# q and k of the second attention stored once in single precision, and split into high and low parts where they are used

## The chip, the core and the metric

The kernel runs on one core of a Trainium2 chip. The metric is the device time of one execution in microseconds. Five engines work side by side, each through its own queue in order: TensorE (PE; its weight loads are shown apart as PEld), VectorE (DVE), ScalarE (ACT), GpSimd (POOL) and SyncE (SP), which here only issues DMAs. They wait for each other by semaphores.

## What is computed

Two layers over 4 sequences of 1024 tokens of width 128. Each layer is an attention with 16 heads and a feed-forward part, both with a residual and a layer norm. The change touches the second attention alone:

```python
q = (x @ Wq).reshape(B, T, H, D)      # B 4, T 1024, H 16, D 64
k = (x @ Wk).reshape(B, T, H, D)
v = (x @ Wv).reshape(B, T, H, D)
q = _rmsnorm(q, q_rms_w)
k = _rmsnorm(k, k_rms_w)
gate = jax.nn.softplus(jnp.einsum('bthd,hd->bht', k, u_n) / math.sqrt(D))
bias = -dist[None, None] * omega_eff[None, :, None, None] * gate[:, :, None, :]
bias = jnp.where(causal[None, None], bias, -jnp.inf)
scores = jnp.einsum('bihd,bjhd->bhij', q, k) * scale + bias
attn = jax.nn.softmax(scores, axis=-1)
y = jnp.einsum('bhij,bjhd->bihd', attn, v).reshape(B, T, H * D)
return y @ Wproj
```

## The kernel before

All tensors are single precision. For q·k the kernel splits each value into a high part, rounded to a type that TensorE multiplies in one pass (`F32R`), and a low part, the rounded rest. The product is then high·high, plus low·high and high·low.

**The projection of the second attention** is the last part of `middle` (`sync_last`, `tensor_last`, `vector_last`, `scalar_last`, lines 1685 to 2014). It goes over 96 items in order: for each of 32 tiles of 128 tokens the items q, k and v. Four tiles are a chunk; there are 8 chunks. Every engine goes through the same numbers n:
- TensorE: `multiply(n)` (line 1783, the product in one of three pairs of banks), then, for item n-3 if it is q or k, two groups of four transposes ("half", line 1742) into one of two banks. After n = 4 of a chunk come the four `aug` transposes of the gates (line 1756), and after n = 8 those of the next chunk's input and the small gate products (lines 1746 and 1752). The two banks are handed on by `free` (line 1759): for a half, when `lower` has read it (semaphore `lows`).
- ScalarE: `root3(n-1)`, then `square(n)` or `keep_v(n)`, then for item n-3 `higher` twice (line 1972), which writes the half times the norm's weight, rounded, into `high`. At n = 2 `soften` (two exponential steps with table loads) for the chunk before, at n = 4 `keep_aug`.
- VectorE: `scale(n-1)` (lines 1843 to 1852), then for item n-3 `lower` twice (line 1864: the half times the weight, minus `high`, into `low`), then `reduce(n)` (line 1836). At n = 3 the gates, at n = 5 `join` and at n = 7 `norm` of the next chunk.
- SP stores `high` and `low` of each q and k item to `s_q1` and `s_k1`, 512 KB each, v to `s_v1`.

**The second attention** is `attend_and_finish`. It goes over `G` = 32 pairs of heads (4 sequences of 8 pairs). A pair has 12 steps u (`units`), each of up to 512 queries against 128 keys: the first four for queries 0 to 511, the other eight for queries 512 to 1023. Steps go in runs of four. For a run TensorE does `scores` of its four steps (lines 564, 565 and the mask, 567), each step followed by `jobs` of the next pairs, and then `values` of the four steps (line 580).
- A job "max" multiplies 128 queries with up to 512 keys (line 537, high parts only) into one of 3 banks (`RING`). VectorE takes the row maximum (lines 631 and 634). `share` says how many jobs follow each step: 3, 2, 1, 1, then 2 each and so on; from step 8 they belong to pair g+2. The maxima of a pair are joined (line 638), transposed (540), negated (640) and laid by a DMA from the ACT queue as one row of `QA` (line 695). `ahead` is what is done before the first score: all maxima of pair 0 and nine of pair 1.
- `scores` writes into 4 banks (`NE`); a step wider than 256 queries takes a bank for each head. ScalarE's `exponentials` (line 690) read them into a ring of 8 `prob` buffers. GpSimd adds these up for the denominators (lines 731 to 735). `keep` (702) and `keep_den` (671) on ScalarE take outputs and denominators out of their banks.
- Operands: `QA` and `KA` hold the high parts in rows 0 to 63 and the position, slope and maximum rows behind them, in 4 buffers (`NA`). `QB` and `KB` hold high and low parts on 128 rows, in 3 buffers (`NB`). `load_a` brings k high, q high and the slopes, `load_b` the four parts for `KB` and `QB` and V. Each of these q and k loads is 512 KB, so a pair takes six of them. A buffer is loaded again when the values of its pair are done.

After the last pair comes the output projection with the last feed-forward part, whose weights and inputs are laid over buffers of the attention that are done with (`over`, `load_last`).

## Time and profile before

| | us |
|---|---|
| median of 3 runs | 2565.62 (2562.55 to 2566.68) |
| the profiled execution | 2563.43 |
| its span, first to last instruction | 2561.3 |
| TensorE busy | 2217.8 |
| VectorE busy | 1378.8 |
| ScalarE busy | 1141.2 |
| GpSimd busy | 682.6 |
| mean granted TensorE clock | 0.922 of 2.4 GHz |

All durations come from the one profiled execution. A granted clock of 0.50 is 1.2 GHz. The projection of the second attention runs from about 873 to 1304 us, the second attention from 1317 to 2151.

### The profile page before, as it was taken

The page shows a single profiled execution, that of the slowest core. Times are in us where ns is not written, and L with a number is a line of the kernel's source. Part 1 is how long each engine was busy: PE and PEld are TensorE (multiplying, and loading weights), DVE is VectorE, ACT ScalarE, POOL GpSimd, SP SyncE. Part 2 cuts the span into 40 slices and gives each one's busy share as a digit, 9 for nine tenths or more (in the row PEclk, how much of TensorE's full clock was granted, in tenths as well). Part 3 has the DMA queues.
Part 4 walks back from the last instruction along what each step waited for, and adds up shares of the span by engine and source line. Part 5 has one row for each costly group of instructions (what it writes and reads, how often), then busy time and mean ns, then how long its engine had stood idle before and what let it go on. Part 6 is the DMA issues. An engine that isn't in the chain of part 4 may idle for free. (4 is left out here: it accounts for less than half of the span.)

```text
span 2561.3 us, 33066 instructions
## 1 busy us (share of the span) xinstructions
PE 2217.8 (87%) x11088; PEld 1286.7 (50%) x11088; DVE 1378.8 (54%) x3484; ACT 1141.2 (45%) x1838; POOL 682.6 (27%) x463
## 2 busy tenths in 40 slices
PE   5499999999839667766749999999999998599998
PEld 2244444444538434333326565656556565355554
DVE  3476766766343476767655555556555553333321
ACT  2145555555525355555534444544444443132322
POOL 5000000000140200000006767676676665000000
PEclk8799999999759888887859999999999999799999
DMA  5724333422227476766698777878787875525300
GB/s 174 201 79 116 128 122 125 92 64 55 93 70 200 115 221 183 216 207 200 200 230 181 172 168 167 175 160 179 163 177 162 181 183 157 141 75 138 84 9 9
DMA packets 339126, 369.66 MB, mean 144 GB/s; under 512 B 22280, under 2 KB 260872, under 8 KB 338573
## 3 DMA queue, kind: packets, MB, share of 16 engines
q1 hardware_dynamic: 321920, 338.45, 52.7%
q0 software_dynamic: 7344, 24.21, 2.7%
q10 hardware_dynamic: 9696, 4.92, 0.8%
q8 instruction: 89, 1.46, 0.3%
q14 instruction: 77, 0.62, 0.1%
HBM read 219.19 MB, written 147.79 MB: 143 GB/s over the span
## 5 line engine op out<-in xcount | busy, mean ns | idle before, releaser
L690 ACT ACTIVATE a1prob<-ps 128x512 f32<-128x512 f32 (+2 forms) x640 | 328.8, 554 | 272.7 <-PE ps L567 242.3
L262 DVE TENSOR_REDUCE a0grid<-ps 128x8 f32<-128x1024 f32 x288 | 346.7, 1223 | 166.3 <-PE ps L171 147.8
L735 POOL TENSOR_TENSOR a1sum<-a1sum,a1prob 128x1024 f32<-128x1024 f32 (+3 forms) x256 | 414.4, 1619 | 78.5 <-ACT a1prob L690 46.3
L319 ACT ACTIVATE a0prob<-ps 128x1024 f32<-128x1024 f32 x288 | 293.6, 1026 | 250.3 <-PE ps L188 219.1
L631 DVE CUSTOM_DVE_ANT_0 ps<-ps,c_mask_ij 128x384 f32<-128x384 f32 (+5 forms) x512 | 273.1, 551 | 230.8 <-issue 226.5
L564 PE MATMUL ps<-a1QA,a1KA 69*128 69x512 f32 (+3 forms) x768 | 283.2, 377 | 8.3 <-DMA a1QA<-a1neg 7.0
L580 PE MATMUL ps<-a1prob,a1V 128*64 128x512 f32 (+3 forms) x1536 | 270.5, 494 | 0.0
L565 PE MATMUL ps<-a1QB,a1KB 128*128 128x512 f32 (+3 forms) x768 | 262.4, 349 | 0.0
L537 PE MATMUL ps<-a1KA,a1QA 68*128 68x384 f32 (+5 forms) x768 | 237.5, 390 | 14.1 <-DMA a1KA<-s_g 13.7
L171 PE MATMUL ps<-a0BK,a0Q 98*128 98x512 f32 x576 | 222.3, 466 | 28.3 <-DMA a0BK<-s_k 25.5
L188 PE MATMUL ps<-a0BQ,a0K 99*128 99x512 f32 x576 | 213.2, 450 | 11.6 <-DVE a0grid L262 9.0
L634 DVE TENSOR_REDUCE a1mx<-ps 128x1 f32<-128x320 f32 (+3 forms) x256 | 150.6, 588 | 109.2 <-PE ps L537 104.9
L580 PEld LDWEIGHTS ps<-a1prob,a1V 128*64 128x64 f32 x1536 | 102.2, 137 | 165.6 <-issue 137.7
L564 PEld LDWEIGHTS ps<-a1QA,a1KA 69*128 69x128 f32 x768 | 148.1, 193 | 53.2 <-issue 45.5
L537 PEld LDWEIGHTS ps<-a1KA,a1QA 68*128 68x128 f32 x768 | 141.8, 199 | 43.0 <-DMA a1KA<-s_g 14.1
L732 POOL TENSOR_TENSOR a1sum<-a1prob 128x768 f32<-128x768 f32 x64 | 134.8, 2106 | 76.3 <-ACT a1prob L690 76.3
L171 PEld LDWEIGHTS ps<-a0BK,a0Q 98*128 98x128 f32 x576 | 103.8, 198 | 98.1 <-issue 41.8
L565 PEld LDWEIGHTS ps<-a1QB,a1KB 128*128 128x128 f32 x768 | 147.6, 192 | 7.5
L203 PE MATMUL ps<-a0prob,a0V 128*32 128x512 f32 (+3 forms) x1536 | 143.9, 492 | 0.1
L188 PEld LDWEIGHTS ps<-a0BQ,a0K 99*128 99x128 f32 x576 | 101.5, 190 | 69.5 <-DVE a0grid L262 53.2
L145 POOL DMA_DIRECT2D s_xs<-c_zero x19 | 13.6, 715 | 410.4 <-DVE y L289 410.4
L1725 POOL DMA_INDIRECT myg<-s_xs,mdest x32 | 30.5, 953 | 327.3 <-DVE macc L1808 216.9
(243 smaller groups left out, 3230.3 us busy)
## 6 DMA issues: line engine op xcount, KB each, us to landing
a1KB<-s_k SPq DMA_DIRECT2D x64, 512.0 KB, 10.6
a1QB<-s_q SPq DMA_DIRECT2D x64, 512.0 KB, 14.1
s_xs<-c_zero POOLq DMA_DIRECT2D x19, 1024.0 KB, 4.5
s_q<-mhi SPq DMA_DIRECT2D x32, 512.0 KB, 3.3
s_q<-mlo SPq DMA_DIRECT2D x32, 512.0 KB, 4.7
s_k<-mhi SPq DMA_DIRECT2D x32, 512.0 KB, 3.3
s_k<-mlo SPq DMA_DIRECT2D x32, 512.0 KB, 4.7
s_v<-mv SPq DMA_DIRECT2D x32, 512.0 KB, 5.4
```

Source lines behind the costliest of these rows:

```text
L171: end = pe.matmul(bank, Q[g % 2][0:NEGROW, t * P:(t + 1) * P], BK[g % 2][0:NEGROW, j, :, :].rearrange("p h n -> p (h n)"), start=True, sto ...
L188: end = pe.matmul(bank, K[g % 2][0:NEGROW + 1, j * P:(j + 1) * P], BQ[g % 2][0:NEGROW + 1, t, :, :].rearrange("p h n -> p (h n)"), start=T ...
L262: dve.tensor_reduce(grid[g % 2][:, a:b + 1:b - a, :], banks(("max", k)), axis=AX.X, op=ALU.max).then_inc(s1_free, 1)
L319: act.activation(prob[:, 2 * u:2 * u + 2, :, :].rearrange("p a h n -> p (a h) n"), banks(("exp", q)), ACT.Exp).then_inc(p_full, 1)
L537: last = pe.matmul(bank[:, 0:j1 - j0], QA[b][0:ROW, h, t * P:(t + 1) * P], KA[b][0:ROW, h, j0:j1], start=True, stop=True)
L564: pe.matmul(s, KA[a][0:ROW + 1, h, keys], QA[a][0:ROW + 1, h, queries], start=k == 0, stop=False)
L565: last = pe.matmul(s, KB[b][:, h, keys], QB[b][:, h, queries], start=False, stop=not diag)
L580: last = pe.matmul(O[h * dim:(h + 1) * dim, off:BANK], V[b][:, j, h * dim:(h + 1) * dim], p[:, h, off:BANK], start=j == 0, stop=u == LAST[c])
L631: dve.tensor_tensor_reduce(bank[:, 0:w], bank[:, 0:w], const["mask_ij"][:, BANK - w:BANK], 1.0, LOWEST, ALU.add, ALU.max, mx[:, x % 2, h, ...
L634: dve.tensor_reduce(mx2[:, x % 2, h, t - IT // 2:t - IT // 2 + 1], bank[:, 0:w], axis=AX.X, op=ALU.max).then_inc(job_free, 1)
L690: act.activation(weights_of(g, u)[:, group[0]:group[-1] + 1, off:BANK], both(e, u, group), ACT.Exp).then_inc(weighed, 1)
L735: pool.tensor_tensor(t[:, :, off:BANK], t[:, :, off:BANK], weights_of(g, u)[:, :, off:BANK], ALU.add).then_inc(summed, 1)
```

## The change

`lower` leaves the projection. `higher` becomes `weigh`, which writes the weighted half as it is (single precision) into `qkT`; SP stores it once. A bank of the transposes is handed on when `weigh` has read it (semaphore `weighted`).

In the attention `load_f(x)` brings k and q of pair x into staging buffers `FK` and `FQ` (two each), twice over, into rows 0 to 63 and 64 to 127: four loads of 512 KB in place of six. `load_e(x)` brings slopes and V. ScalarE's `split(x, k)`, for k = 0 to 3 (k and q, head 0 and 1), copies 128 rows by 1024 into `KB` or `QB`, rounded, and 64 rows by 1024 into `KA` or `QA`. VectorE's `lower(x, k)` then overwrites 64 rows of `KB` or `QB` with the staged values minus the rounded ones. For pair g+2, `split` stands behind `exponentials` of steps 0 to 3 of pair g, and `lower` ahead of the maxima of steps 2 to 5. For pairs 0 and 1, `split` stands ahead of everything on ScalarE, `lower(0, k)` ahead of the first maximum, and `lower(1, k)` behind maxima 8 to 11. `QA` and `KA` have 3 buffers. The weights of the last part lie over the staging buffers.

```diff
-            for buf, r0, src in ((KA, 0, heads_of(x, "k1", 0)), (QA, 0, heads_of(x, "q1", 0)), (KA, EXT, slopes)):
...
-            for buf, r0, src in ((KB, 0, heads_of(x, "k1", 1)), (KB, dim, heads_of(x, "k1", 0)),
-                                 (QB, 0, heads_of(x, "q1", 0)), (QB, dim, heads_of(x, "q1", 1))):
...
+        def load_f(x):
+
+            b = x % 2
+            if x > 1:
+                nc.sync.wait_ge(rounded, SPLIT * (x - 1))
+                nc.sync.wait_ge(lowered, LOW * (x - 1))
+            for buf, name in ((FK, "k1"), (FQ, "q1")):
+                for r in range(2):
+                    nc.sync.dma_start(buf[b][r * dim:(r + 1) * dim, :, :], heads_of(x, name)).then_inc(loaded_f[b], 16)
...
             for g in range(G + 1):
+                if g + 3 < G:
+                    load_f(g + 3)
                 if g > 0:
-                    if g - 1 + NA < G:
-                        load_a(g - 1 + NA)
-                    if g - 1 + NB < G:
-                        load_b(g - 1 + NB)
+                    if g + 2 < G:
+                        load_e(g + 2)
...
                     if k == 0:
-                        pe.wait_ge(loaded_a[b], (x // NA + 1) * 16 * N_A)
+                        pe.wait_ge(loaded_e[b], (x // NB + 1) * 16)
+                        pe.wait_ge(rounded, SPLIT * (x + 1))
...
                 if u == 0:
-                    pe.wait_ge(loaded_b[b], (g // NB + 1) * 16 * N_B)
-                    pe.wait_ge(row_in[a], (g // NA + 1) * 16)
+                    pe.wait_ge(loaded_v[b], (g // NB + 1) * 16)
+                    pe.wait_ge(lowered, LOW * (g + 1))
+                    pe.wait_ge(row_in[b], (g // NB + 1) * 16)
...
+            def lower(x, k):
+
+                which, h = divmod(k, 2)
+                buf, wide, lines = (FK, KB, slice(dim, P)) if which == 0 else (FQ, QB, slice(0, dim))
+                dve.wait_ge(rounded, SPLIT * x + 2 * k + 1)
+                dve.tensor_tensor(wide[x % NB][lines, h, :], buf[x % 2][lines, h, :], wide[x % NB][lines, h, :].bitcast(F32), ALU.subtract).then_inc(lowered, 1)
...
             for g in range(G):
                 for u in range(NU):
+                    if g + 2 < G and 2 <= u < 6:
+                        lower(g + 2, u - 2)
...
+            def split(x, k):
+
+                which, h = divmod(k, 2)
+                buf, wide, narrow = (FK, KB, KA) if which == 0 else (FQ, QB, QA)
+                if k == 0:
+                    act.wait_ge(loaded_f[x % 2], (x // 2 + 1) * 64)
+                    if x >= NB:
+                        act.wait_ge(valued, unit(x - NB, NU - 1) + 1)
+                act.activation(wide[x % NB][:, h, :], buf[x % 2][:, h, :], ACT.Copy).then_inc(rounded, 1)
+                act.activation(narrow[x % NB][0:dim, h, :], buf[x % 2][0:dim, h, :], ACT.Copy).then_inc(rounded, 1)
...
                     exponentials(g, u)
+                    if g + 2 < G and u < 4:
+                        split(g + 2, u)
...
-                    sp.wait_ge(lows, 4 * tile + 2 * kind + 2)
-                    for part, buf in enumerate((high, low)):
+                    sp.wait_ge(weighted, 4 * tile + 2 * kind + 2)
...
-                    pe.wait_ge(lows, 2 * nth(a) + b + 1)
+                    pe.wait_ge(weighted, 2 * nth(a) + b + 1)
...
-                dve.scalar_tensor_tensor(low[tile % 2][:, kind, to, :], view, wn[:, 0:1], high[tile % 2][:, kind, to, :].bitcast(F32),
-                                         ALU.mult, ALU.subtract).then_inc(lows, 1)
...
-                act.activation(high[tile % 2][:, kind, half * 4:half * 4 + 4, :], view, ACT.Copy, scale=(wqn, wkn)[kind][:, 0:1]).then_inc(highs, 1)
+                act.activation(qkT[tile % 2][:, kind, half * 4:half * 4 + 4, :], view, ACT.Copy, scale=(wqn, wkn)[kind][:, 0:1]).then_inc(weighted, 1)
```

## Rows read from the trace of the kernel before

**Rows 1.** Busy time by stage: length, busy us (count) of each engine, granted clock, DMA share, GB/s.

```profile
core 0: us, PE busy (x) PEld busy (x) DVE busy (x) ACT busy (x) POOL busy (x), PEclk, DMA share, GB/s
860.00:1300.00 440.00, 302.46 (x1020) 165.44 (x1020) 293.46 (x521) 230.93 (x358) 28.70 (x31) 0.82 0.67 199
1320.00:1325.00 5.00, 4.72 (x11) 2.84 (x10) 4.97 (x24) 0.00 (x0) 0.00 (x0) 0.50 1.05 212
1363.00:2118.00 755.00, 750.39 (x4212) 453.69 (x4208) 431.16 (x1738) 361.23 (x688) 521.90 (x329) 1.00 0.78 173
1614.49:1639.72 25.23, 25.12 (x143) 15.16 (x141) 14.37 (x58) 12.09 (x24) 17.49 (x12) 1.00 0.78 171
```

**Rows 2.** The same view, one projection chunk, cut at its key multiplies.

```profile
1128.98:1138.21 9.23, 7.33 (x31) 3.78 (x29) 8.12 (x11) 5.25 (x9) 0.00 (x0) 1.00 0.64 182
1138.21:1147.92 9.71, 7.45 (x28) 3.86 (x28) 8.14 (x12) 5.64 (x10) 0.00 (x0) 1.00 0.90 269
1147.92:1165.45 17.53, 10.91 (x32) 6.00 (x33) 11.37 (x28) 10.65 (x16) 0.00 (x0) 0.71 0.74 226
1165.45:1183.55 18.10, 12.84 (x42) 7.59 (x41) 9.20 (x16) 7.56 (x14) 0.00 (x0) 0.72 0.49 146
```

**Rows 3.** Groups in that chunk (1123.78:1178.30): busy us, mean ns | idle before, releaser.

```profile
L1836 DVE TENSOR_REDUCE mss<-msq 128x16 f32<-128x1024 f32 x8 | 9.7, 1208 | 0.0
...
L1864 DVE SCALAR_TENSOR_TENSOR mlo<-ps,mwqn,mhi 128x512 fp32r<-128x512 f32 x8 | 5.7, 746 | 14.7 <-ACT mhi L1972 14.7
...
L1972 ACT ACTIVATE mhi<-ps,mwqn 128x512 fp32r<-128x512 f32 x8 | 5.2, 687 | 0.0
```

**Rows 4.** TensorE in order of time, one pair's first run: start, length, [idle before].

```profile
1625.82 0.50 PE L564 MATMUL ps<-a1QA,a1KA 69*128 69x512 f32 x1
...
1630.67 2.38 PE L580 MATMUL ps<-a1prob,a1V 128*64 128x512 f32 x16
1632.97 0.50 PE L564 MATMUL ps<-a1QA,a1KA 69*128 69x512 f32 x1
```

**Rows 5.** ScalarE in order of time, the same run's exponentials.

```profile
1626.73 1.11 ACT L690 ACTIVATE a1prob<-ps 128x512 f32<-128x512 f32 x2 [0.20 <-PE ps L567]
1628.49 0.89 ACT L690 ACTIVATE a1prob<-ps 128x384 f32<-128x384 f32 x2 [0.65 <-PE ps L567]
1629.91 1.09 ACT L690 ACTIVATE a1prob<-ps 128x512 f32<-128x512 f32 x2 [0.54 <-PE ps L567]
```

**Rows 6.** Single lines over the whole span: durations ns least/median/most, first and last start.

```profile
L679 ACT CAST a1KA<-a1kpos x8: 1034/1036/1043, 1312.0 to 1318.6; 5x1024 fp32r<-5x1024 f32 x8
L1120 DVE TENSOR_TENSOR p0low<-p0full,p0high x16: 680/684/4079, 23.6 to 90.2; 128x512 fp32r<-128x512 f32 x16
L1852 DVE TENSOR_TENSOR mqk<-ps,mss x64: 1215/1221/1226, 879.7 to 1293.0; 128x1024 f32<-128x1024 f32 x64
L638 DVE TENSOR_TENSOR a1mx<-a1mx x32: 166/1422/1706, 1330.6 to 2119.6; 128x8 f32<-128x8 f32 x32
```

**Rows 7.** GpSimd and VectorE in order of time at the end of one pair's maxima.

```profile
1638.76 2.36 POOL L735 TENSOR_TENSOR a1sum<-a1sum,a1prob 128x1024 f32<-128x1024 f32 x1
...
1639.72 1.42 DVE L638 TENSOR_TENSOR a1mx<-a1mx 128x8 f32<-128x8 f32 x1
```

**Rows 8.** ScalarE and TensorE in order of time at the start of the second attention.

```profile
1312.02 7.66 ACT L679 CAST a1KA<-a1kpos 5x1024 fp32r<-5x1024 f32 x8 [7.58 <-DMA a1kpos<-in_kpos]
...
1317.52 12.09 PE L537 MATMUL ps<-a1KA,a1QA 68*128 68x128 f32 x24 [13.70 <-DMA a1KA<-s_g]
...
1342.26 0.77 PE L564 MATMUL ps<-a1QA,a1KA 69*128 69x512 f32 x1 [6.95 <-DMA a1QA<-a1neg]
```

**Rows 9.** TensorE in order of time in the projection chunk: start, length, [idle before].

```profile
1138.21 1.98 PE L1783 MATMUL ps<-mwk,mflip 128*128 128x512 f32 x4 [1.63 <-DVE mqk L1852]
...
1145.26 1.04 PE L1742 MATMUL ps<-c_ident,mqk 128*128 128x128 f32 x8
...
1152.62 1.82 PE L1742 MATMUL ps<-c_ident,mqk 128*128 128x128 f32 x8 [2.71 <-DVE mlo L1864]
...
1159.26 3.62 PE L1783 MATMUL ps<-mwv,mflip 128*128 128x512 f32 x4
```

More of the change, by code:

```diff
@@ L365, in attend_and_finish @@
     early = sum(share[TURN:])
-    assert G % NA == 0 and sum(share) == NM
+    assert sum(share) == NM
     def jobs(g, u):
@@ L408, in over @@
             return nc.alloc_sbuf_tensor_at(f"f{name}", shape, F32, offset=spot[place] + 4 * offset)
-        QA, KA, QB, KB = ([own(f"{n}{b}", [P, 2, S], F32R) for b in range(NA if n[1] == "A" else NB)] for n in ("QA", "KA", "QB", "KB"))
+        QA, KA, QB, KB = ([own(f"{n}{b}", [P, 2, S], F32R) for b in range(NB)] for n in ("QA", "KA", "QB", "KB"))
+        FQ, FK = ([own(f"{n}{b}", [P, 2, S]) for b in range(2)] for n in ("FQ", "FK"))
         V = [own(f"V{b}", [P, IT, P]) for b in range(NB)]
@@ L415, in attend_and_finish @@
         den = [own(f"den{r}", [P, BANK]) for r in range(2)]
-        qpos, kpos = own("qpos", [P, S]), own("kpos", [P, S])
+        qpos, kpos = (prob[r][:, :, :].rearrange("p h n -> p (h n)") for r in range(2))
         ones = own("ones", [P, 32])
@@ L524, in job @@
                 kind, x, k = order[d]
-                b, bank = x % NA, SD[d % RING]
+                b, bank = x % NB, SD[d % RING]
                 if d >= RING:
@@ L676, in scalar_program @@
             act.wait_ge(c_in, 16 * 2)
-            for b in range(NA):
+            for b in range(NB):
                 for h in range(2):
@@ L702, in keep @@
                 act.activation(raw[x % 2][c][:, :], O, ACT.Copy).then_inc(o_kept, 1)
+            def split(x, k):
[7 more added lines that the diff above has]
+                act.activation(narrow[x % NB][0:dim, h, :], buf[x % 2][0:dim, h, :], ACT.Copy).then_inc(rounded, 1)
+            for x in range(2):
+                for k in range(4):
+                    split(x, k)
             row(0)
@@ L1209, in middle @@
         qk, v = [own(f"qk{r}", [P, HD]) for r in range(3)], [own(f"v{r}", [P, HD]) for r in range(2)]
-        high, low = ([own(f"{n}{r}", [P, 2, PAIRS, P], F32R) for r in range(2)] for n in ("hi", "lo"))
+        qkT = [own(f"qkT{r}", [P, 2, PAIRS, P]) for r in range(2)]
         z, zabs, g, gj = [own(f"z{r}", [P, TILES, heads]) for r in range(2)], own("zabs", [P, TILES, heads]), own("g", [P, TILES, heads]), own("gj", [P, TILES, heads])
@@ L1901, in vector_last @@
                     scale(n - 1)
-                if n >= TLAG and kinds(n - TLAG)[1] != WV:
-                    lower(n - TLAG, 0)
-                    lower(n - TLAG, 1)
                 if n < NI and kinds(n)[1] != WV:
@@ L2056, in build @@
             ("ident", [P, P], F32), ("identb", [P, P], BF16), ("mask_ji_add", [P, P], BF16), ("mask_ij", [P, BANK], BF16),
-            ("ones", [P, 1], F32), ("zero", [P, BANK], F32), ("above", [P, BANK], BF16), ("below", [P, BANK], BF16))}
+            ("ones", [P, 1], F32))}
+        front = ctx.enter_context(ExitStack())
+        const.update({n: sbuf(nc, front, f"c_{n}", [P, BANK], d) for n, d in (("zero", F32), ("above", BF16), ("below", BF16))})
         c_in, c_set = nc.alloc_semaphore("c_in"), nc.alloc_semaphore("c_set")
```

109 lines of the change are left out of this document (51 added, 58 removed).

## The prediction

> **What bounds the kernel now.** I began with the table of busy times by stage [rows 1]. The change touches two stages: the projection of the second attention (860 to 1300 us) and the second attention itself (1363 to 2118 us). In the second attention TensorE is busy for 750.39 of 755 us at a granted clock of 1.00. One pair of heads takes 25.23 us, in which VectorE works 14.37 us, ScalarE 12.09 and GpSimd 17.49. The reader is to see that TensorE has no spare time there and ScalarE has 13 us a pair: any new stall is paid in full, and nothing can be gained, whatever is taken from the DMA queues. In the projection no engine is full. VectorE is the busiest (293 of 440 us), the granted clock is 0.82, and the stage is held by a chain that passes from engine to engine.
>
> So I cut one chunk of the projection (12 items, four tiles, 54.6 us) into the intervals from one key multiply to the next [rows 2]: 9.23, 9.71, 17.53 and 18.10 us. The first two are ordinary tiles; the third holds the gates with their table loads and the `aug` transposes; the fourth holds `join`, `norm` and the transposes of the next chunk. In the last two the clock falls to 0.71 and 0.72.
>
> **The projection: what is removed.** VectorE's `lower` (128 instructions, 0.746 us each) goes, and with it VectorE's idle time before it, 14.7 us in a chunk [rows 3]: `lower` waited for ScalarE, which had itself waited. A transposed half now leaves its bank after ScalarE's 0.687 us [rows 3]. I walked the chunk with the same durations in the new order of instructions:
> - Ordinary tile: VectorE keeps two reductions (1.21) [rows 3], two reciprocals and two scalings (1.22) [rows 6], each pair with a 0.4 us wait for ScalarE's root: about 6.3 us. TensorE has three multiplies of 1.75 us start to start and two groups of transposes of 0.9: 7.0 us, and becomes the bound. 9.23 and 9.71 become 7.0 and 7.0: 2.2 and 2.7 us less.
> - Gates tile: table loads and exponentials on ScalarE stay in series with square, weighing and the transposes; two `lower` pairs and their waits go. The walk gives 14.3 for 17.53: 3.2 us less. TensorE still stands before `aug` for 2.6 us, so I leave the value multiply after it at the slow length, 3.62 [rows 9].
> - Last tile: 14.7 for 18.10: 3.4 us less, with the multiply after the next chunk's transposes still slow.
> Eight, eight, seven and seven times: 18 + 22 + 22 + 24 = 86 us, and about 3 us at the drain, where the last `lower`s stand before the gates: 89 us. If the shorter stalls keep the clock up behind `aug` and the transposes, another 3.8 us a chunk comes back. Bounds: 70 to 120 us. The 64 stores of 512 KB that go with it (32 MB) I cost at nothing: the DMA share is 0.67 there [rows 1] and nobody's wait in [rows 2] names a store. The weighing waits for a store of two tiles before, some 14 us old.
>
> **The second attention: what is added on ScalarE.** Eight copies of 1024 elements a pair, two behind each of the first four exponential steps. Nearest row: the 1024-element cast from SBUF to the rounded type, 1.036 us [rows 6]; back to back eight of them took 7.66 [rows 8], so 0.95 each from start to start. Two put 1.9 us behind each step. The walk, from the start of a pair's first score (1625.82) [rows 4]: ScalarE now ends the exponentials of steps 0 to 3 at about 2.0, 3.6, 4.7 and 5.2 [rows 5]. With the copies between them they end at 2.0, 4.7, 7.1 and 9.3. TensorE starts the values at 4.85 and ends them at 7.15 [rows 4]; step 2 must now wait until 7.2, and step 3 until 9.4. TensorE stands 0.8 and 1.7 us, **2.5 us a pair**. The fourth pair of copies and the keeping of the output then end at 11.7, and the next exponentials follow just in time for the fifth and sixth scores: 0 to 0.4 us more.
>
> **On VectorE**, four subtractions of 1024 elements with both inputs in SBUF, before the maxima of steps 2 to 5. Nearest rows: 0.684 us for 512 elements of this very form and 1.221 us for 1024 with one input in PSUM; I take 1.22 [rows 6]. They also meet GpSimd. The 8-element `tensor_tensor` of line 638 takes 0.166 us at its shortest and 1.422 at the median [rows 6]; the one at 1639.72 ends at 1641.14, just as GpSimd's addition ends (1638.76 + 2.36) [rows 7]. So a subtraction waits for the addition in progress, and the other way round. That is what the Trainium skill says, in SBUF — State Buffer, section "SBUF: two separate sides": VectorE with two SBUF inputs and a GpSimd instruction lock one port pair for a whole instruction. The trace agrees, 1.422 against 0.166. Queued behind the subtractions are the maxima, and TensorE waits for these with a ring of three banks. In the walk the first subtraction is free (GpSimd has nothing yet), the second and third wait about 1.3 us each beneath TensorE's own stall, the fourth ends at 13.3, and TensorE loses 0.4 us at the maxima of step 6. Bounds 0 to 2.0.
> Sum: 2.9 us for each of 30 pairs (the last two have no pair to split for) = **87 us**; bounds 2.2 (copies that overlap as the casts did, nothing lost on VectorE) to 3.6 a pair, 66 to 108.
>
> **Loads.** q and k come four times instead of six (a pair's 3 MB become 2), a third buffer replaces the fourth of the narrow operands, and `load_e` is queued behind `load_f` on SP. A pair's load is issued more than a pair (25 us) ahead and takes some 10 us. Nothing there, neither a gain nor a loss; if SP's queue were late the cost would show as a wait of the first maxima.
>
> **The start of the stage.** The first score work now needs 2 MB instead of 1 (at 212 GB/s [rows 1], 5 us more), then eight copies (7.7 us), which were not there, less 1.9 for the two casts of line 679 that the fourth buffer took: the first maxima slip by about 10 us from 1317.5 [rows 8]. Later the maxima of the second pair wait for its own load and split, but ahead of the first scores TensorE already stood 6.95 us for the 8 KB row of negated maxima, behind bulk loads [rows 8]. I take 10 us; bounds 3 to 18.
>
> **The clock.** New stalls can lower it. Before: a stand of 1.63 us leaves the next multiply at 1.98, one of 2.71 leaves the transposes at 1.82 instead of 1.04; after the gates' stalls the multiply takes 3.62 [rows 9], which is the lower level, 1.2 GHz for 2.4. The new pattern, 2.5 us standing with half a microsecond of work inside it, lies between. A fall costs about 2 us a time, half of some 4 us until the clock is back (the multiply at 1159.26 was slow through its end at 1162.9). I take a third of the pairs: 20 us; bounds 0 and 75.
>
> **Sum** against the profiled execution's own 2563.4 us (its span 2561.3 and 2.1 around it): 2563.4 − 89 + 87 + 10 + 20 = 2591. It lies 2.2 us below the median of the runs, 2565.62, so about **2593** as a median; slower by 1.1%.
>
> **The rivals.**
> 1. *The projection's chain gives more, and the attention's clock holds* (faster). If TensorE, standing under 2 us before `aug` and the transposes, stays at 2.4 GHz, a chunk falls to 39 us: 8 × 15 = 120 us. With the clock held in the attention too and 2.5 us a pair: 2566 − 120 + 75 + 8 = 2529. It decides from about 25 us more than I gave to the projection or less than I took for the attention. For it: in [rows 2] ordinary tiles run at 1.00. Against: 2.6 us before `aug` remain, as long as the stand that now lowers it.
> 2. *The clock falls in every pair*: 2.5 us or more at 1.2 GHz, 75 us instead of 20: 2648. For it: [rows 9], 2.71 us was enough. Against: 1.63 was not.
> 3. *The port pair decides*: every subtraction waits for a full addition of 2.4 us and VectorE, 14.4 + 4 × 3.6 = 28.8 us a pair, becomes the bound: 3.6 to 5 us a pair, 30 × 1.5 = 45 us more: 2638. This is also what the rule named above would give if GpSimd always held the pair first. The rows leave open who comes first when both wait. Against: GpSimd is idle 7.7 of 25.23 us, and the subtractions stand where it starves.
> 4. *Both sums cancel*: within 5 us, the clock holding and the start hidden: 2566.
>
> **How the numbers follow.** Forecast 0.44, rival 1 0.22, rival 2 0.13, rival 3 0.09, rival 4 0.12. For the range I go from 2530 (rival 1) to 2650 (rival 2), which leaves out about 2 in 10. Some 0.2% (5 us) is what a measurement of this kernel can tell from no change: faster 0.23, same 0.12, slower 0.65.
>
> **What would show it.** Right: `lower` gone and projection intervals of 7.0, 7.0, 14 and 15 us; a pair of 28 us with TensorE waiting for ScalarE at line 580's weights of steps 2 and 3; subtractions of 1.2 us, some stretched to 2.5; a granted clock below 1.00 only here and there in the attention. Wrong: a pair at 25.2 (the copies hidden), a pair over 30 (clock or port), or a projection chunk still at 50 us, which would mean that another wait, of the stores or of the gathered rows, stands behind `lower`.

## The result and the profile after

| | before | after |
|---|---|---|
| median of the runs | 2566.15 us (2562.55 to 2570.53) | 2725.36 us (2719.93 to 2728.84, 4 runs) |
| ratio | | 1.0618, 95% interval 1.0593 to 1.0642 |
| span of the profiled execution | 2561.3 | 2718.1 |
| TensorE busy | 2217.8 | 2329.1 |
| VectorE busy | 1378.8 | 1482.9 |
| ScalarE busy | 1141.2 | 1372.8 |
| mean granted clock | 0.922 | 0.882 |

The change made the kernel 6.2% slower. The forecast was 1.1% slower, 2593 us, with a range of 2530 to 2650: the sign was right, the size was not. The span grew by 156.8 us, and three places in the trace make this up: the projection ends 102.8 us earlier, the start of the attention takes 16.4 us more, and the attention with what follows it takes 243 us more.

**The projection.** The view of busy time by windows, of after, one chunk cut at its key multiplies. It answers to [rows 2]; the order of the four intervals is gates, last tile, two ordinary tiles. Columns as in [rows 1].

```profile
1041.83:1056.38 14.55, 10.34 (x35) 5.41 (x34) 8.65 (x23) 10.27 (x16) 2.18 (x3) 0.77 0.55 173
1056.38:1069.02 12.64, 10.34 (x43) 6.01 (x41) 6.50 (x12) 6.81 (x13) 1.62 (x2) 0.87 0.45 141
1069.02:1075.92 6.90, 6.90 (x31) 3.93 (x29) 5.39 (x7) 5.85 (x10) 0.00 (x0) 1.00 0.55 158
1075.92:1082.82 6.90, 6.90 (x30) 3.94 (x29) 5.52 (x8) 6.19 (x10) 0.00 (x0) 1.00 0.72 228
```

A chunk went from 54.6 us to 41.0. In the ordinary tiles TensorE is busy for the whole interval. TensorE in order of time in the same chunk, answering to [rows 9]:

```profile
1049.16 1.12 PE L1791 MATMUL ps<-c_ident,maug 128*128 128x128 f32 x4 [2.45 <-ACT mqkT L1992]
1050.07 3.62 PE L1818 MATMUL ps<-mwv,mflip 128*128 128x512 f32 x4
...
1062.37 0.63 PE L1781 MATMUL ps<-c_ident,mxout 128*128 128x128 f32 x4 [1.52 <-DVE mxout L1862]
```

TensorE stands 2.45 us before `aug`, and the value multiply behind it still takes 3.62 us. Before the next chunk's input it now stands only 1.52 us, and those transposes run at full speed (0.63); the clock falls right behind them, and the multiply at 1064.98 still takes 3.33 us.

**The attention.** The window view of the stage, which answers to the third line of [rows 1], where TensorE was busy for 750.39 of 755 us at a clock of 1.00:

```profile
1300.00:2250.00 950.00, 848.66 (x3971) 500.81 (x3969) 578.21 (x1751) 544.26 (x873) 545.99 (x311) 0.84 0.40 95
```

TensorE now stands idle for 101 of 950 us and its clock averages 0.84. Who it stands for, from the view of waits of the same stretch (us in all, times, longest):

```profile
PE ps L569 <- DMA a1QA<-a1neg: 95.7, 27, 4.2
```

The view of the tile `QA` has the row's issues, and the time from issue to landing (least/median/most):

```profile
L712 ACTq DMA_DIRECT2D a1QA<-a1neg x32: 510/510/629, 1247.5 to 2282.8; - x32
DMA to landing us min/median/max: 1.8/8.1/8.9
```

It is the 8 KB row of negated maxima, once in nearly every pair. Before, the same row landed in 1.8/1.9/10.5 us. One pair in order of time: SP's queue, the row's issue on ScalarE's queue, and TensorE.

```profile
1713.12 1.07 SPq L480 DMA_DIRECT2D s_den<-a1den  x2
1714.29 1.29 SPq L453 DMA_DIRECT2D a1FK<-s_k  x2
1715.63 1.25 SPq L453 DMA_DIRECT2D a1FQ<-s_q  x2
...
1719.16 0.51 ACTq L712 DMA_DIRECT2D a1QA<-a1neg  x1
...
1721.70 2.38 PE L585 MATMUL ps<-a1prob,a1V 128*64 128x512 f32 x16
1727.44 0.77 PE L569 MATMUL ps<-a1QA,a1KA 69*128 69x512 f32 x1 [3.37 <-DMA a1QA<-a1neg]
...
1736.14 4.35 PE L585 MATMUL ps<-a1prob,a1V 128*64 128x512 f32 x16
```

The reader is to see the order of issue. `load_f(g + 3)` is written at the head of SP's iteration, but its waits were met long ago, so it goes out as soon as SP is through with the iteration before, which ends with the denominators of step 7. Two megabytes are then on their way when ScalarE issues the row. The second `FQ` load, issued at 1716.27, lands at 1727.17 and the row at 1727.20, and the first score starts at 1727.44. In each of the 27 pairs counted above, TensorE's first score starts 0.24 to 0.28 us after its row has landed. The trace agrees with what the Trainium skill says in DMA: Bandwidth & Descriptors, section "Queues, rings and completion order": queues of different engines share the same DMA engines, and a semaphore's increment lands only after every earlier write of its DMA engine, across the queues. Whether the row's own bytes are late or only its increment, no run here shows.

And then the clock. The pair's first run goes at a granted 0.50, so the 16 value multiplies take 4.35 us where [rows 4] has 2.38. At that speed TensorE is so slow that ScalarE's copies, the stall I had predicted, are hidden.

To put a number on the clock I cut the stage of each kernel into single microseconds and counted those with a granted clock below 0.75, and the times the clock fell. The length of a pair is the time from the first row's issue to the last, divided by 31 (so it holds a 31st of what the first and the last pairs take). Idle is the stretch less TensorE's busy time. Such a table is used for all runs below.

| kernel | stretch, us | TensorE idle | us at low clock | falls | pair, us |
|---|---|---|---|---|---|
| before | 700 | 3 | 0 | 0 | 25.6 |
| after | 950 | 101 | 294 | 28 | 33.4 |

A stretch of 950 us is 28.4 pairs: 3.6 us standing and 10.3 us at 1.2 GHz a pair. Work done at half the clock takes twice as long, so 10.3 us cost about 5.2. Both together are 8.7 us. Inside the stretches a pair, from one row's issue to the next, takes 33.9 us against 25.25, so it grew by 8.6; the 7.8 in the table is less because the first and the last pairs, which it also holds, grew less. Only 6 of the 294 low microseconds were also idle. The Trainium skill describes the pattern in TensorE: Matmul & The Clock Gate, section "HAM oscillation — how this bites in real kernels": a wait for a DMA in every round of a loop makes each round start slow. The trace agrees, with 28 falls in 28 pairs.

### The profile page after: what moved, and what is told of

The parts are those of the page before. It is cut to its first block, busy times and chain, and to the rows that moved or that the text cites. A ratio compares the mean times of both kernels' runs of the same rounds, so it can differ in the third digit from the quotient of the medians.

```text
span 2718.1 us, 33231 instructions
## 1 busy us (share of the span) xinstructions
PE 2329.1 (86%) x11040; PEld 1349.1 (50%) x11088; DVE 1482.9 (55%) x3482; ACT 1372.8 (51%) x2092; POOL 737.1 (27%) x463
## 3 DMA queue, kind: packets, MB, share of 16 engines
q8 instruction: 90, 1.47, 0.2%
## 4 chain that ended last, share of the span: by engine, by line
PE 34%; DMA 10%; issue 6%; DVE 4%; ACT 1%; SPq 0%; ACTq 0%; DVEq 0%
DMA a1QA<-a1neg 8%; PE ps L933 8%; PE ps L569 5%; PE ps L585 5%; PE ps L570 5%; PE ps L541 5%; PE ps L884 2%; DVE a1mx L643 1%; PE ps L572 1%; PE ps L944 1%; PE ps L922 1%; DMA frec<-s_rec 1%; PE ps L921 1%; DVE a1mx L639 1%; DMA a1FQ<-s_q 1%
## 5 line engine op out<-in xcount | busy, mean ns | idle before, releaser
L768 POOL TENSOR_TENSOR a1sum<-a1sum,a1prob 128x1024 f32<-128x1024 f32 (+3 forms) x256 | 460.8, 1800 | 90.6 <-ACT a1prob L707 61.9
L569 PE MATMUL ps<-a1QA,a1KA 69*128 69x512 f32 (+3 forms) x768 | 317.1, 417 | 100.5 <-DMA a1QA<-a1neg 100.5
L585 PE MATMUL ps<-a1prob,a1V 128*64 128x512 f32 (+3 forms) x1536 | 319.6, 566 | 4.0 <-ACT a1prob L707 4.0
L541 PE MATMUL ps<-a1KA,a1QA 68*128 68x384 f32 (+5 forms) x768 | 280.1, 443 | 32.9 <-ACT a1QA L730 26.2
L570 PE MATMUL ps<-a1QB,a1KB 128*128 128x512 f32 (+3 forms) x768 | 296.4, 390 | 0.0
L569 PEld LDWEIGHTS ps<-a1QA,a1KA 69*128 69x128 f32 x768 | 174.2, 227 | 148.8 <-issue 140.1
L188 PE MATMUL ps<-a0BQ,a0K 99*128 99x512 f32 x576 | 213.5, 451 | 14.9 <-DVE a0grid L262 14.3
L541 PEld LDWEIGHTS ps<-a1KA,a1QA 68*128 68x128 f32 x768 | 162.7, 230 | 72.9 <-issue 26.6
L570 PEld LDWEIGHTS ps<-a1QB,a1KB 128*128 128x128 f32 x768 | 173.9, 226 | 9.3
L764 POOL COPY a1sum<-a1prob 128x256 f32<-128x256 f32 x32 | 15.0, 469 | 433.9 <-ACT a1prob L707 433.8
L657 DVE TENSOR_TENSOR a1KB<-a1FK,a1KB 64x1024 fp32r<-64x1024 f32 x64 | 124.1, 1938 | 11.4 <-ACT a1KB L729 9.6
```

The lines of the kernel that those rows point to most:

```text
L188: end = pe.matmul(bank, K[g % 2][0:NEGROW + 1, j * P:(j + 1) * P], BQ[g % 2][0:NEGROW + 1, t, :, :].rearrange("p h n -> p (h n)"), start=T ...
L541: last = pe.matmul(bank[:, 0:j1 - j0], QA[b][0:ROW, h, t * P:(t + 1) * P], KA[b][0:ROW, h, j0:j1], start=True, stop=True)
L569: pe.matmul(s, KA[b][0:ROW + 1, h, keys], QA[b][0:ROW + 1, h, queries], start=k == 0, stop=False)
L570: last = pe.matmul(s, KB[b][:, h, keys], QB[b][:, h, queries], start=False, stop=not diag)
L585: last = pe.matmul(O[h * dim:(h + 1) * dim, off:BANK], V[b][:, j, h * dim:(h + 1) * dim], p[:, h, off:BANK], start=j == 0, stop=u == LAST[c])
L768: pool.tensor_tensor(t[:, :, off:BANK], t[:, :, off:BANK], weights_of(g, u)[:, :, off:BANK], ALU.add).then_inc(summed, 1)
```

## The experiments

All edits are to the kernel after unless another is named. The kernel before ran beside each group of them, with medians of 2564.7 to 2570.2 us, so medians from different groups can differ by some 5 us without a cause in the edits.

### The loads at the start of a pair

```diff
                 if g + 3 < G:
+                    if g > 0:
+                        nc.sync.wait_ge(valued, unit(g - 1, NU - 1) + 1)
                     load_f(g + 3)
```

> The changed kernel with one line more: SyncE waits for the last values of pair g-1 before it issues the staging loads of pair g+3, so they start at the pair's start as in the kernel before, and not at step 7, just ahead of the 8 KB row of negated maxima. Theory (queued row): the row lands about 2 us after its issue, TensorE's 3.4 us stand before the first score of each pair and the half-speed stretch behind it go, and what stays is the walk of the prediction, about 28 us a pair: 2570 to 2600 us. Rival (the copies and subtractions cost it, the row only fills a gap that would be there anyway): no more than 30 us less, 2695 us or above.

2672.92 us (2663.09 to 2678.19, 4 runs), ratio 1.0395 (1.0368 to 1.0422). The row's landing is back at 1.8 us (median), and its waits are gone from the pairs. But only 52 us came back. What is left, in TensorE's order of time, is the predicted stall, and behind it the clock:

```profile
1706.64 1.72 PE L587 MATMUL ps<-a1prob,a1V 128*64 128x512 f32 x8
1708.88 0.65 PE L587 MATMUL ps<-a1prob,a1V 128*64 128x256 f32 x4 [0.51 <-ACT a1prob L709]
1711.04 0.54 PE L587 MATMUL ps<-a1prob,a1V 128*64 128x128 f32 x4 [1.51 <-ACT a1prob L709]
...
1721.41 1.94 PE L553 MATMUL ps<-a1sum,a1ones 128*32 128x512 f32 x8
1723.28 4.44 PE L587 MATMUL ps<-a1prob,a1V 128*64 128x512 f32 x16
```

The stands are 0.51 and 1.51 us at steps 2 and 3 (I had 0.8 and 1.7). The denominators of step 7, ten microseconds later, take 1.94 us; in the kernel before they took 1.06. In windows:

```profile
1640.00:1645.00 5.00, 2.98 (x19) 1.04 (x18) 4.81 (x9) 5.00 (x8) 4.58 (x3) 1.00 1.04 215
1645.00:1650.00 5.00, 5.00 (x19) 4.09 (x16) 4.53 (x12) 4.14 (x7) 2.62 (x3) 0.64 1.11 242
1650.00:1655.00 5.00, 5.00 (x19) 3.01 (x17) 2.46 (x7) 2.39 (x4) 4.71 (x3) 0.50 0.14 51
1655.00:1660.00 5.00, 5.00 (x25) 1.29 (x18) 1.57 (x3) 0.60 (x1) 1.58 (x1) 0.84 0.01 2
```

TensorE works without a gap from 1645 on, and still has 1.2 GHz until about 1656. Counted as above: of 900 us 60 idle, 269 at the low clock, 25 falls in 28 pairs. So a fall lasts 10.8 us in the mean and costs about 5.4. The mean hides a spread: of the 25 falls 17 last about 14 us, four about 10 and four about 3, behind the same two stands.

2672.92 us is still above the 2650 at which the prediction's range ended. With the loads held back the price of the clock is enough to carry the time out of it.

### The kernel before with q's and k's loads behind step 7

```diff
                 if g > 0:
                     store_den(g - 1)
+                    if g - 1 + NB < G:
+                        load_b(g - 1 + NB)
```

(of `load_b` the four loads of q and k; V stays where it was)

> The kernel before, with no splitting, but its four 512 KB loads of KB and QB moved from the pair's start to behind the store of the denominators (step 7), ahead of the row of maxima. Theory (queued row): the same 3 to 4 us stand before the first score of each pair, a fall of the clock behind it, a pair of 31 to 34 us, 2740 to 2850 us in all. Rival (the late row needs the splitting to hurt): 2566 us as before, within 10.

2812.45 us (one run), 242 us above the 2570.2 of before beside it, with no copy and no subtraction added. The row's landing:

```profile
L705 ACTq DMA_DIRECT2D a1QA<-a1neg x32: 510/511/629, 1328.6 to 2374.2; - x32
DMA to landing us min/median/max: 1.8/7.9/9.4
```

TensorE, of the same kernel:

```profile
1707.53 0.47 PE L574 MATMUL ps<-a1QA,a1KA 69*128 69x512 f32 x1 [3.01 <-issue]
```

The view of waits puts these stands down to "issue" and not to the row, but the traces decide it: the first score starts 0.09 to 0.14 us after the row has landed, in every pair that stands. Of 940 us 93 idle, 336 at the low clock, 28 falls. The place of the bulk loads alone costs the kernel before as much (242 us) as the whole change costs the attention and what follows it (243). That the two numbers agree so closely is chance: the change also adds the copies, whose stall is hidden there.

### Half of the loads late

```diff
             for buf, name in ((FK, "k1"), (FQ, "q1")):
+                if name == "q1" and x > 3:
+                    nc.sync.wait_ge(valued, unit(x - 4, NU - 1) + 1)
```

> The kernel after with k's loads (1 MB) where they are, behind the denominators of step 7, and q's (1 MB) at the start of a pair. Theory (the row of negated maxima lands once the bulk bytes issued before it are through, and TensorE has some 4.7 us of cover for it): the row lands at 4 to 5 us in place of 8.1, hardly anything waits for it, and the time is that of the run with all four loads at the pair's start, 2655 to 2700 us. Rival (a row behind any bulk load lands as late as behind two megabytes): 2710 to 2730.

2670.88 us (one run), the row at 1.8/3.0/8.7 us. As the theory had it, if quicker than its 4 to 5 us: with one megabyte ahead the row is in time, and the kernel is as fast as with all loads at the pair's start. In most pairs the row lands 0.2 us after the last load ahead of it.

### Without VectorE's subtractions

The kernel with the loads at the pair's start, without `lower` for pairs 2 to 31; the low parts are left out of those scores.

```diff
-                    if g + 2 < G and 2 <= u < 6:
-                        lower(g + 2, u - 2)
```

> The kernel of e1 without VectorE's subtractions for pairs 2 to 31: the low parts of k and q are left out of the scores there. Theory (VectorE's subtractions cost TensorE 0.4 us a pair, as walked): 5 to 25 us less than e1. Rival (the port pair decides): 50 us or more less than e1.

2666.41 us (one run), 6.5 us less than the median with them. That lies inside the 2663 to 2678 over which the four runs with them spread, so it is 0.2 us a pair at the face of it and cannot be told from nothing, nor from the 0.4 I had. The 50 us or more of the rival are excluded. Where the subtractions stand here, beneath TensorE's own stall, VectorE and its port are not what costs.

### The copies alone, in the kernel before

```diff
                     exponentials(g, u)
+                    if g + 2 < G and u < 4:
+                        for r in range(2):
+                            act.activation((qpos, kpos)[r][:, :], KB[g % NB][:, 0, :].bitcast(F32), ACT.Copy)
```

(the waits between the copies are left out here)

> The kernel before with ScalarE's part of the change alone: two copies of 128 rows by 1024 behind each of the exponential steps 0 to 3 of pairs 0 to 29, out of a loaded buffer into two that nothing reads any more. Nothing else is touched; the result is the same. Theory (the copies alone bring the stands of 0.5 and 1.5 us and the falls of the clock of the run with the loads at the pair's start, 2.1 + 4.8 us a pair): 30 x 6.9 = 207 us more, 2750 to 2790 us. Rival (the falls of the clock need the subtractions or the new loads beside the copies): 30 x 2.1 to 30 x 2.9, 2625 to 2655.

2769.52 us (one run), 203 us more than before. The two waits of a pair and the clock behind them:

```profile
1666.39 0.65 PE L581 MATMUL ps<-a1prob,a1V 128*64 128x256 f32 x4 [0.53 <-ACT a1prob L691]
1668.56 0.44 PE L581 MATMUL ps<-a1prob,a1V 128*64 128x128 f32 x4 [1.51 <-ACT a1prob L691]
...
1677.75 1.94 PE L548 MATMUL ps<-a1sum,a1ones 128*32 128x512 f32 x8
```

Eight copies at that place need nothing else of the change to cost 6.8 us a pair, of which 2.1 are stands (60 of 900 us idle) and the rest clock (288 us low, 24 falls).

### Four copies early, four later

Based on the kernel with the loads at the pair's start, as are the next three.

```diff
-                    if g + 2 < G and u < 4:
-                        split(g + 2, u)
+                    if g + 2 < G:
+                        for k in {0: (0, 1), 1: (2, 3), 4: (4,), 5: (5,), 6: (6,), 7: (7,)}.get(u, ()):
+                            split(g + 2, k)
...
-                    if g + 2 < G and 2 <= u < 6:
-                        lower(g + 2, u - 2)
+                    if g + 2 < G and u in (2, 3, 6, 8):
+                        lower(g + 2, (2, 3, 6, 8).index(u))
```

(k now counts single copies)

> As the run with one copy a step, but two copies behind each of steps 0 and 1, none behind 2 and 3, and one behind each of steps 4 to 7; subtractions ahead of the maxima of steps 2, 3, 6 and 8. The first half of the stall alone is left: the exponentials of step 2 end at 7.1 us, the values want them at 6.2, so TensorE stands some 0.5 to 0.9 us a pair, once, and not the 1.5 us behind it. Theory (it is the length of the stands close together that brings the clock down): the clock holds in nearly all pairs, 2500 to 2540 us. Rival (any stand in this place brings it down): 60 to 90 us less than the run with the loads at the pair's start, 2580 to 2640.

2514.26 us (one run), 159 us less than with eight. The first stand is still there:

```profile
1665.23 0.87 PE L587 MATMUL ps<-a1prob,a1V 128*64 128x256 f32 x8 [0.51 <-ACT a1prob L709]
```

and the clock does not move, by the window view of the stage (no microsecond of it at the low clock):

```profile
1300.00:2040.00 740.00, 716.65 (x3937) 419.70 (x3938) 583.83 (x1732) 522.40 (x864) 574.90 (x308) 1.00 0.55 123
```

Taking away the second stand, 1.51 us, took 159 us off, of which 30 × 1.5 = 45 us are the stand itself; the rest is mostly the clock, whose 269 low microseconds had cost about 135. Inside the stretch a pair takes 26.5 us, 1.3 more than the 25.25 of before: 0.5 is the stand that is left, 0.2 are small waits for maxima, and the rest is not explained. Two subtractions and four copies moved with it, but only to places where TensorE waits for neither.

### One copy a step

```diff
-                    if g + 2 < G and u < 4:
+                    if g + 2 < G and u < 8:
                         split(g + 2, u)
...
-                    if g + 2 < G and 2 <= u < 6:
-                        lower(g + 2, u - 2)
+                    if g + 2 < G and u in (2, 4, 6, 8):
+                        lower(g + 2, u // 2 - 1)
```

> The kernel after with its loads at the start of a pair (as in the run that took 2673 us), and ScalarE's eight copies put one behind each of the exponential steps 0 to 7 in place of two behind each of steps 0 to 3; the subtractions move with them, ahead of the maxima of steps 2, 4, 6 and 8. Theory (what is left of the loss is TensorE's stand for ScalarE in steps 2 and 3, 0.51 and 1.51 us, and the fall of the clock that follows it, which I count in 25 of 28 pairs with 269 us at 1.2 GHz out of 900): with one copy of 0.95 us behind a step the exponentials of steps 0 to 3 end at 2.0, 3.85, 5.4 and 6.7 us, and the values, which start at 4.85, need steps 2 and 3 at 6.2 and 6.7, so nothing is left to stand for; in the second run the exponentials end at 2.0, 4.1, 6.2 and 8.2, in time as well. 60 us of stands and some 135 us of clock go: 2470 to 2520 us, clock near 1.00 in the stage. Rival (the copies take ScalarE's time wherever they stand, and VectorE's subtractions meet GpSimd): 2580 to 2680.

2598.58 us (2595.91 to 2602.76), ratio 1.0132 (1.0114 to 1.0150). The theory's range, up to 2520, was missed by 79 us; the time lies in the rival's, which had named both the copies and the subtractions. The waits for ScalarE are gone, as it said, but two for maxima have come. TensorE, VectorE and GpSimd of this kernel, in order of time:

```profile
1675.71 1.66 DVE L659 TENSOR_TENSOR a1KB<-a1FK,a1KB 64x1024 fp32r<-64x1024 f32 x1
...
1677.95 0.44 PE L543 MATMUL ps<-a1KA,a1QA 68*128 68x384 f32 x1 [0.96 <-DVE a1mx L641]
...
1678.31 2.40 POOL L769 TENSOR_TENSOR a1sum<-a1prob 128x1024 f32<-128x1024 f32 x1 [2.02 <-ACT a1prob L709]
...
1679.30 2.49 DVE L659 TENSOR_TENSOR a1QB<-a1FQ,a1QB 64x1024 fp32r<-64x1024 f32 x1
...
1682.38 0.50 PE L543 MATMUL ps<-a1KA,a1QA 68*128 68x512 f32 x1 [1.47 <-DVE a1mx L641]
```

The subtraction at 1679.30 falls into GpSimd's addition (1678.31 to 1680.71) and lasts 2.49 us instead of 1.2. The maxima queued behind it come late, and with three banks TensorE has to wait. Of 820 us 72 are idle and 60 low, in 18 falls of only 3.3 us each.

### The subtractions at other steps

```diff
-                    if g + 2 < G and u in (2, 4, 6, 8):
-                        lower(g + 2, u // 2 - 1)
+                    if g + 2 < G and u in (2, 3, 8, 9):
+                        lower(g + 2, (2, 3, 8, 9).index(u))
```

> The kernel with one copy a step (2598.6 us), with VectorE's subtractions ahead of the maxima of steps 2, 3, 8 and 9 in place of 2, 4, 6 and 8. In the trace of that kernel TensorE waits 0.96 and 1.47 us a pair for maxima in steps 5 and 7, behind the subtractions of steps 4 and 6, which VectorE begins while GpSimd adds 1024 elements. Theory (these two waits, and the clock's falls behind them in 18 of 28 pairs, are all that is left; ScalarE's copies cost nothing where they stand): 28 x (2.4 + 1.1) = 98 us less, 2490 to 2520 us. Rival (one copy a step delays ScalarE itself, and the maxima only show it): 2570 to 2600.

2611.42 us (2606.11 to 2612.29), ratio 1.0170 (1.0150 to 1.0190). Missed: instead of a gain of 98 us, 13 us more. The waits had only moved, to one of 1.95 and one of 0.65 us a pair; of 830 us 76 are idle and 95 low, in 21 falls. The subtraction ahead of step 9 meets an addition as well, and a wait of 1.95 us stands behind it:

```profile
1669.83 2.69 DVE L659 TENSOR_TENSOR a1QB<-a1FQ,a1QB 64x1024 fp32r<-64x1024 f32 x1
...
1673.26 0.79 PE L543 MATMUL ps<-a1KA,a1QA 68*128 68x384 f32 x2 [1.95 <-DVE a1mx L638]
```

So far it was argued, not shown, that the subtractions and not ScalarE make these maxima late. The next run decides it.

### One copy a step, no subtractions

The kernel with one copy a step, without `lower` for pairs 2 to 31, so again without the low parts in those scores.

> The kernel with one copy a step (2598.6 us) without VectorE's subtractions for pairs 2 to 31: the low parts of those pairs are left out of the scores. In that kernel, and in the one with the subtractions ahead of steps 2, 3, 8 and 9 (2611 us), TensorE waits for maxima that are queued behind a subtraction, and the subtraction lasts 2.3 to 2.8 us where GpSimd is adding, 1.2 where it is not. Theory (the subtractions, waiting for GpSimd's additions, cost all of the 2.4 us a pair and the clock's falls behind them): 28 x 3.5 = 98 us less, 2485 to 2515 us, and the copies, one a step, cost nothing. Rival (VectorE's maxima are late because ScalarE's copies shift the whole pair): 2560 to 2600.

2472.29 us (one run), 126 us less, and 13 us below the theory's range. The stage is as dense as before the change:

```profile
1300.00:2000.00 700.00, 696.98 (x3916) 420.68 (x3911) 418.25 (x1614) 517.86 (x858) 485.24 (x306) 1.00 0.57 129
```

Eight copies a pair, one a step, cost nothing that can be measured (25.5 us a pair). The same four subtractions, worth 6.5 us or nothing where TensorE stood anyway, are worth 126 us where it did not.

### The projection's half alone

In the kernel before, `lower` is taken out of the projection, and TensorE and SP wait for ScalarE's `highs` in place of `lows`. All stores stay, 64 of them of a tile set once, so the low parts are left out of the result.

> The kernel before with the projection's half of the change alone: VectorE's subtraction of the high parts leaves the projection, and a bank of transposes is handed on when ScalarE has read it. The low parts are left out of the result: zeros, set once, are stored in their place, so the 64 stores of 512 KB and all loads of the attention stay as they were. Theory: the projection's gain is in its chain of engines and not in its stores, 102.8 us as between the traces of before and after, and the attention keeps its 25.2 us a pair: 2455 to 2475 us. Rival (a good part of those 102.8 us came from the 32 MB that are no longer stored): 2490 to 2530.

2474.29 us (one run), 90.4 us less than the 2564.68 beside it. The theory gave 2455 to 2475 us, so it sits just at the edge. Where most of the difference to 102.8 is, TensorE's order of time at the end of the projection shows:

```profile
1204.86 1.08 PE L1758 MATMUL ps<-c_ident,maug 128*128 128x128 f32 x4 [5.91 <-DVEq L1883]
1225.00 12.09 PE L537 MATMUL ps<-a1KA,a1QA 68*128 68x128 f32 x24 [19.05 <-DMA a1KA<-s_g]
```

The stage ends at 1204.86, 97.9 us earlier than before, and in the kernel after at 1199.95. From the last transposes to the first maxima it is then 20.1 us, where [rows 8] with the end of the projection at 1302.73 gives 14.8. The 64 stores are thus worth 4.9 us in the stage and 5.3 behind it, about 10 together. What most of the 5.3 are, SP's queue shows. The first load of the attention's inputs goes out when the last store has landed, and that is 9.0 us after the start of the last transposes here (1213.87) and 4.1 in the kernel before (1306.83): with the same stores in a shorter stage they land later than the arithmetic ends.

### The copies in ScalarE's gaps

This version was set down together with the first three runs, before the later ones: the bulk loads behind the row, the copies where ScalarE has time, the subtractions where VectorE has.

```diff
                 if g > 0:
                     if g + 2 < G:
                         load_e(g + 2)
...
                     store(g - 1, 1)
+                if g + 3 < G:
+                    load_f(g + 3)
...
-                    if g + 2 < G and u < 4:
-                        split(g + 2, u)
+                    if g + 2 < G and u == 3:
+                        for k in range(0 if g == 0 else 2, 4):
+                            split(g + 2, k)
+                    if g + 3 < G and u == 11:
+                        for k in range(2):
+                            split(g + 3, k)
...
+                    if g + 2 < G and u == 2 * TILES - 1:
+                        for k in range(4, 8):
+                            split(g + 2, k)
```

(k = 0 to 3 are the narrow copies, which the maxima need first, 4 to 7 the wide ones; the subtractions stand behind steps 7, 11, 11 and 3)

> The changed kernel with the loads issued after the pair's start, and ScalarE's eight copies moved into its idle time: the narrow ones behind steps 11 and 3, the wide ones behind step 7; the subtractions go behind steps 7, 11 and 3. Theory (it is the place that costs, not the work): 25.3 to 26.5 us a pair at full clock, and the projection's gain stays: 2475 to 2520 us. Rival (the volume costs: VectorE and ScalarE too full): as e1 or above, 2560 us or more.

2501.53 us (2501.02 to 2502.11, 4 runs), ratio 0.9741 (0.9725 to 0.9758): faster than both kernels. Its attention is not quite as dense as before (17 of 730 us idle, 10 low, 26.4 us a pair for 25.6), which costs about 25 us of the projection's gain.

### The same, with the first row ahead of the third pair's loads

```diff
+            nc.sync.wait_ge(row_in[0], 16)
             load_f(2)
             load_e(2)
```

> The version with the copies in ScalarE's gaps (2501.5 us), with the loads of the third pair held until the first row of negated maxima has landed. There TensorE stands 3.52 us for that row, which takes 7.0 us behind two megabytes. Theory: it lands in 1.8 and the stand goes, 3 to 5 us less, 2495 to 2500 us. Rival (the third pair's loads, now later, are late for ScalarE's copies behind step 3 of the first pair): no gain, 2500 to 2508.

2505.21 us (2502.77 to 2505.57), ratio 0.9760 (0.9743 to 0.9777). No gain. The stand of 3.52 us before the first score is gone, as the theory had it, and waits for maxima of 1.12 and 0.51 us take its place in the first two pairs. The 3.7 us between the two versions are too little to tell them apart: they were measured in different groups, the intervals of their ratios overlap, and in the profiled execution the projection had already ended 2.6 us later.

## Why the prediction failed where it did

**Loads: "Nothing there, neither a gain nor a loss".** This is the step that failed. I had looked at whether a load would be late, and SP's queue as something that can only be behind. The question was the other one: when does it now issue, and what small transfer is on its way at that time? In before the loads waited for the values of the pair that freed their buffers, which put them behind that pair's rows by accident. With staging buffers freed at step 5 that wait is gone. The evidence lay in [rows 8]: TensorE stood 6.95 us for the 8 KB row behind bulk loads, and I used it for the start of the stage only. Price: moving the loads back gives 52 us; their place alone, in the kernel before, costs 242. The two do not add up with the copies' 203, because both make TensorE stand, and the clock falls once a pair whichever it is.

**The clock: "a third of the pairs", "about 2 us a time".** Mis-sized in both factors. With the row's wait out of the way it falls in 25 of 28 pairs and stays low for 10.8 us, so 5.4 us a time: some 135 us for the 20 I took, and nearly twice the 75 of rival 2. My 2 us came from one multiply in the projection that was slow for 4 us [rows 9]. The trace of before had better rows. In [rows 2] a mean clock of 0.71 over 17.53 us is 10.2 us at the low level, and 0.72 over 18.10 us is 10.1. And at the start of the attention the clock, down since 1293, did not come back under dense work for 12 us, from the first score at 1342.26 to about 1354:

```profile
1345.00:1350.00 5.00, 5.00 (x21) 4.10 (x19) 3.06 (x15) 1.89 (x4) 1.75 (x2) 0.50 1.05 210
1350.00:1355.00 5.00, 5.00 (x21) 2.20 (x21) 1.03 (x5) 0.42 (x2) 2.42 (x3) 0.58 1.15 190
```

([rows 1] show a piece of the same stretch, 4.72 of 5 us busy at 0.50.) Ten us at the low level cost up to 5, which with a fall in every pair would have been up to 150 us. Rival 2 was right that stands of 2 us with little between them are enough; it had the price wrong too.

**The copies' stall: 2.5 us a pair.** Right. Walked 0.8 and 1.7, measured 0.51 and 1.51; 60 idle us in 28 pairs are 2.1. A copy takes 1.045 us (1.036 from the cast). In the kernel after it is hidden, because TensorE runs that part at half speed.

**The subtractions: 0.4 us a pair, beneath TensorE's own stall.** Not contradicted where they stood (0.2, inside the spread of the runs). They take 1.21 us alone, as expected; those of the keys have a median of 1.43 and reach 2.84. Rival 3, the port pair, did not decide in this kernel. But the condition I named, "beneath TensorE's own stall", carried the whole term: with the stall taken away and one copy a step they cost 126 us with the clock.

**The projection: 89 us.** 102.8. The intervals of 7.0, 7.0 and 14.3 were measured as 6.90, 6.90 and 14.55, the last tile as 12.64 for 14.7, as the shorter stand (1.52 us) leaves the clock up in the transposes. Half of rival 1 came true, 14 us of its 31. "The stores I cost at nothing" was wrong by about 10 us. The [rows 2] that the text leans on hold no waits at all, and without the stores the stage ends 4.9 us earlier and the next begins sooner.

**The start: 10 us.** 16.4: the first maxima come 27.3 us after the projection's end instead of 14.8, the first score after 55.9 instead of 39.5. Within the bounds (3 to 18), at their upper part, since the last maxima of the first pair wait for the second pair's copies and the row stands 4.73 us again.

With the stands and the clock as measured, the sum would have been, for the loads held: 2563.4 − 102.8 + 16.4 + 30 × (2.1 + 4.8) = 2684, where the profiled execution took 2678.2 (median 2672.9); and for the kernel after, with 3.6 and 5.2 a pair, 2741, where it took 2719.9 (median 2725.4). The second is 21 us too high, since not all 30 pairs grew by 8.7 us.

## What to carry to other kernels

When a wait is removed from a load, ask at what time it will now be issued, and which small, urgent transfer, on any queue, is then behind it: 8 KB behind 2 MB took 8.1 us instead of 1.9. Where TensorE runs dense at full clock, price a stand not by its length but with the clock behind it: one of 0.5 us a pair left the clock up, and 0.5 and 1.5 us in quick succession cost 7. Take the length of a fall from the trace you have, where the clock fell for any reason. And "hidden beneath a stall" is a price that holds only as long as the stall; put each piece where its engine has time of its own.

## What the runs showed of the hardware that I had not expected

- The clock, once down, can stay at 1.2 GHz for 14 us although TensorE works without a gap all the while. What stood before the falls, and how long they lasted:

| kernel | stands of a pair, us | falls in the stretch | each at the low clock, about us |
|---|---|---|---|
| four copies early | 0.51 | 0 | |
| copies in the gaps | 0.97 to 0.99, in three of 28 pairs | 2 | 7 and 3 |
| one copy a step | 0.96 and 1.47, 5.4 us from the first's start to the second's end | 18 | 3 |
| subtractions elsewhere | 1.96, and 0.65 long after | 21 | 3 or 7 |
| loads at the pair's start | 0.51 and 1.51, within 2.7 us | 25 | 14, 10 or 3 |
| after | one of 3.2 to 4.2 | 28 | 10, some 14 or 7 |

  Each stretch holds 28 pairs. Single stands of 0.51 us never brought the clock down, and stands of 2 us or more in all did in most pairs. But the stands alone do not decide how long a fall lasts, nor whether there is one; what does is open. In the pair from 1606 to 1625 us of the run with the loads at the pair's start it did not fall at all, with the same two stands:

```profile
1610.00:1615.00 5.00, 4.49 (x31) 2.64 (x29) 4.86 (x15) 5.00 (x8) 2.73 (x2) 1.00 1.02 224
1615.00:1620.00 5.00, 3.49 (x21) 2.64 (x18) 4.75 (x10) 5.00 (x9) 3.69 (x3) 1.00 1.07 203
```

- The row's landing against the bulk issued ahead of it, 2 to 6 us before: none 1.8 us, one megabyte 3.0, two 8.1 (7.9 in the kernel before with its loads moved). In most pairs it landed within 0.4 us of the last of the loads.
- A subtraction that starts while GpSimd adds lasts until the addition is through and then about its own time: 2.49 us in place of 1.2 where the addition had 1.41 us to go, and 2.5 to 2.8 in 59 of the 128 subtractions with one copy a step. This agrees with the rule of SBUF — State Buffer in the Trainium skill, section "SBUF: two separate sides", that whichever of the two starts first has the shared port pair for the whole instruction; the price behind it is the 126 us above.
